# Moving VectorE's normals, low parts and the raw copies between the places of a quad of attention heads

## The chip, the cores and the metric

One Trainium2 chip; the program runs on one of its cores. The metric is the device time of one execution in microseconds, as the median over runs. Lower is better.

## What is computed

A transformer block on x of shape (8, 512, 256) in float32: layernorm, 16-head attention with l2-normalized queries and keys, an output projection, layernorm and residual; then a feed-forward block with ternary weights, layernorm and residual. Cut to what matters:

```python
q = l2norm(x @ w_q) * exp(scale);  k = l2norm(x @ w_k)      # 16 heads of 64
attn = softmax(einsum('bhid,bhjd->bhij', q, k))
out = einsum('bhij,bhjd->bhid', attn, v) @ w_out + b_out
x = x + layernorm(out)
h = silu(x1 @ w1 * s1) * (x1 @ w2 * s2)                     # x1 = layernormed x
h = gelu(h @ h1 * t1);  h = gelu(h @ h2 * t2)
x = x + layernorm(h @ w3 * s3)
```

## The kernel before

TensorE multiplies in a rounded float32 format. To keep float32 precision each operand is split in a high part (the rounded value) and a low part (what is left), and products of high with high, high with low and low with high are added up. So nearly every tile that TensorE reads has a high part, made by ScalarE or GpSimd with a copy, and a low part, made by VectorE with a subtraction.

Attention runs as a pipeline over 256 slots (two per head, `i` in the code), and a few more at its end. Eight slots, called places 0 to 7 here (`r = i % 8`), serve a quad of four heads, which is two pairs of heads: an even pair, then an odd one. There are 32 quads. Every engine has its own program: a loop over the slots, in which the order of the calls is written out by hand. Each engine works strictly in that order, and waits on semaphores.

What TensorE does in a slot: scores of slot i (L1027, L1028, into a pair of PSUM banks), values of slot i - 2 (L1044, six matmuls, reading `Ph` and `Pl`), and then, by place: in places 6, 0, 1 and 2 a projection of one tile of x to queries and keys (L986), in 3 and 4 one to values, in 0 and 5 the transposes of a pair's keys and queries ("turn", L1013), in 7 the output projection of the quad before last (`outp`, L1058). Those results go to three banks `G`, which a plan hands out in order; each user waits until the one before it on the bank is evacuated (`wait_bank`). In place 1 the projection gets the bank that held the turned keys of place 0, in place 2 that of the turned queries.

What the other engines do for it. Slot by slot ScalarE computes exp (L493) and its high part `Ph` (L498), VectorE the low part `Pl` (`p_low`, L705) of the slot before; the values matmuls one slot later want it. ScalarE squares a projected tile (L472), VectorE sums it (`head_sums`, L675), GpSimd takes the root (L362, L365, L368), VectorE scales the tile (`head_scale`, L684). Turned keys and queries are split by ScalarE (L485) and VectorE (`turn_low`, L699), then SP's queue copies them into the operand layout of the scores (`stack`, L245 and L246, 640 KB for each head of the pair; the scores wait for them, and so does the next `turn_high`).

The softmax sums go another way. ScalarE evacuates a head's values and sum (`evacuate`, L504); SP moves the sum into `Dp` (`take_sums`, L254, 2 KB); VectorE takes the reciprocal of a pair (`invert`, L713, places 7 and 3); SP stores it in HBM (`store_rec`, L259, "rows<-Rp") and reads it back spread over partitions (`spread_rec`, L266, "work<-rows"); VectorE multiplies (`normal`, L721, two instructions, a pair's result is called its normals), GpSimd copies the high part (`o_high`, L373), VectorE subtracts for the low part (`o_low`, L727), and `outp` reads both. `add_part` (L739) adds the projection to y. In place 7 VectorE does the scale of place 6's tile, then `invert`, then two `add_part`; then, in place 0, `p_low`.

ScalarE's queue also issues copies of 22 pieces of the raw feed-forward weights inside HBM (`copy_piece`, L509, 512 KB each), one at the end of place 7 of each quad up to slot 183, and 22 loads with which VectorE counts nonzero bits (`look_piece`, `count_piece`, L764), at the end of fixed slots. All SP transfers share one queue, ScalarE's another.

After the slots come the feed-forward layers (`layers`, `group`, `gate`, `halves`), for eight batches.

Of the kernel before, what the change touches and what calls it, by code (L numbers as in the profile page):

```python
# [15 lines left out]
NP = B * HP  # L16
NQ = B * 4
NU = 2 * NG
# [158 lines left out]
PIECES = 22  # L177
# [9 lines left out]

def copy_at(i):

    n, r = divmod(i - 15, 8)  # L190
    return n if r == 0 and 0 <= n < PIECES else None

# [26 lines left out]
def sync_program(q, M):  # L219
# [80 lines left out]
    for i in range(SLOTS):  # L300
        g, c, b, r, live = slot(i)
        i32_, pb = i % 32, i // 32 - 1
        if i in (5, 6):
            load_wo(i - 3)
        if i % 2 == 0 and 0 <= i // 2 - 2 < NG:
            take_sums(i // 2 - 2)
        if i % 4 == 0 and 0 <= i // 4 - 2 < NP:
            spread_rec(i // 4 - 2)
        if 0 <= pb < B - 1 and i32_ == 16:
            store_x1(pb)  # L310
        if pair_of(i) is not None:
            stack(pair_of(i), 0)
        late = 2 if i % 8 == 2 else 1
        if i >= late and i % 8 in (2, 6) and pair_of(i - late) is not None:
            stack(pair_of(i - late), 1)
        if i % 4 == 3 and 0 <= i // 4 - 1 < NP:
            store_rec(i // 4 - 1)
        if i == 3:
            load_x(1)
        if b + 2 <= B and i32_ == 31:  # L320
            load_x(b + 2)
        if 0 <= pb and i32_ == 6:
            load_xr(pb)
# [15 lines left out]
def pool_program(q, M):  # L339
# [68 lines left out]
    for i in range(SLOTS):  # L408
        g, c, b, r, live = slot(i)
        i32_, pb = i % 32, i // 32 - 1  # L410
        if b < B and i32_ == 5:
            norm_root(b + 1)
        if i % 4 == 1 and 0 <= i // 4 - 2 < NP:
            o_high(i // 4 - 2)
# [30 lines left out]
def act_program(q, M):  # L445
# [120 lines left out]
    for i in range(SLOTS):  # L566
# [20 lines left out]
        if i == NU:  # L587
            q.wait_ge("cst", 64)
            e.activation(M.pre[:, :], M.sc["s1"][:, 0:1], ACT.Silu).then_inc(S["pre"])
        if copy_at(i) is not None:  # L590
            copy_piece(copy_at(i))
        if i in LOOKS:
# [29 lines left out]
def vector_program(q, M):  # L622
# [244 lines left out]
    for i in range(NU + 1):  # L867
# [6 lines left out]
        if 0 <= i - 1 < NU:  # L874
            p_low(i - 1)
        if r == 1 and pair_of(i - 1) is not None:
            turn_low(pair_of(i - 1), 1)
            turn_low(pair_of(i - 1), 0)
        if i < 3:
            split_w(4 + i)  # L880
        if i in (5, 6, 12, 13):
            split_wo(i - 5 if i < 7 else i - 10)
        if i % 4 == 2 and 0 <= n - 3 < NP:
            o_low(n - 3)
        if i % 4 == 1 and 0 <= n - 3 < NP:
            normal(n - 3)
# [13 lines left out]
        if values_of(i) is not None:  # L900
            v_low(values_of(i))
        if r == 5 and pair_of(i) is not None:
            turn_low(pair_of(i), 1)
            turn_low(pair_of(i), 0)
        for u in tiles_of(i - 1) if i else []:
            head_scale(u)
        if r == 7 and 0 <= n - 2 < NP:
            invert(n - 2)
# [7 lines left out]
        if i == FLAG_AT + 1:  # L916
            flag()
    normal(NP - 2)
    for b in range(B):
        for n in range(3):  # L920
            for m in range(KH):
# [9 lines left out]
                elif m:  # L931
                    halves(b, n, m - 1)
                if b == 0 and n == 0 and m in (0, 1):
                    add_part(NQ - 2, m)
                if b == 0 and n == 0 and m == 2:
                    o_low(NP - 2)
# [33 lines left out]
def tensor_program(q, M):  # L970
# [171 lines left out]
    def layers(b, rounded):  # L1142

        for n in range(3):
            for m in range(KH):
                group(b, n, m, rounded)
                if b == 0 and n == 1 and m == 1:
                    outp(NQ - 1, 0)
                    outp(NQ - 1, 1)
        if b + 1 < B:  # L1150
            turn3(b + 1)
        last_tiles(b, rounded)
# [20 lines left out]
    def rest(rounded):  # L1173

        for i in range(BRANCH_AT, NU + 2):
            attention(i)
        outp(NQ - 2, 0)
        outp(NQ - 2, 1)
        for b in range(B):
            layers(b, rounded)  # L1180
# [205 lines left out]
```

## Time and profile before

| what | value |
|---|---|
| runs | 1758.13 us median of 3 (1755.85 to 1760.71) |
| the profiled execution | 1754.84 us, of which the span of its instructions is 1753.0 us |
| TensorE busy | 1701.9 us, 97% of the span |
| VectorE busy | 1179.5 us, 67% (8 tenths in most slices of the attention stage, 5 later) |
| ScalarE busy | 1009.9 us, 58% |
| GpSimd busy | 497.6 us, 28% |
| TensorE's granted clock | 0.995 of full speed |
| the chain that ended last | PE 76%, DVE 10%, DMA 6% |

PE is TensorE, DVE VectorE, ACT ScalarE, POOL GpSimd, SP the sync engine, whose instructions here only issue transfers. A row of a timeline gives the start and the length of an instruction (x2: of two together) and, in brackets, the idle time of its engine before it and what ended that. Attention takes the first 1085 us or so, the feed-forward layers the rest.

### The profile page before, as it was taken

The numbers are of one execution on the slowest core, as the hardware profiler recorded it, in microseconds if no ns is written. First come the engines' busy times: TensorE is split into PE (matmuls) and PEld (weight loads), VectorE is DVE, ScalarE is ACT, GpSimd is POOL, SyncE is SP. The second block draws the span as 40 slices with busy tenths as digits, with TensorE's granted clock in tenths as the row PEclk, the third lists the DMA queues.
The fourth block names the chain that finished last, engine by engine and source line by source line (L and its number), as shares of the span: only waits on it lengthen the run. The fifth ranks groups of instructions, "written<-read, shape, count | busy, mean of one in ns | idle before, by whom it ended". The sixth has DMA issues, their size and how long they took to land.

```text
span 1753.0 us, 24640 instructions
## 1 busy us (share of the span) xinstructions
PE 1701.9 (97%) x8578; PEld 1414.8 (81%) x8578; DVE 1179.5 (67%) x2022; ACT 1009.9 (58%) x1350; POOL 497.6 (28%) x561
## 2 busy tenths in 40 slices
PE   5999999999999999999999998999999999999998
PEld 4778888888878888888888886888888888888877
DVE  5777887887877887887887885545454545544454
ACT  4777777777777777777777775322323141323231
POOL 3533543543543543543543540000000000000000
PEclk9999999999999999999999999999999999999999
DMA  4546546546546546546546654400000000000000
GB/s 129 121 113 163 135 115 164 133 117 164 131 115 163 133 118 163 131 115 157 116 108 152 175 138 105 166 13 24 1 25 1 25 1 24 1 25 1 25 1 24
DMA packets 76780, 163.41 MB, mean 93 GB/s; under 512 B 28272, under 2 KB 28656, under 8 KB 76656
## 3 DMA queue, kind: packets, MB, share of 16 engines
q1 hardware_dynamic: 67296, 128.64, 30.9%
q10 hardware_dynamic: 8352, 29.50, 5.7%
q0 software_dynamic: 1008, 3.67, 0.5%
q8 instruction: 71, 1.16, 0.3%
q14 instruction: 53, 0.43, 0.1%
HBM read 68.97 MB, written 20.19 MB: 51 GB/s over the span
## 4 chain that ended last, share of the span: by engine, by line
PE 76%; DVE 10%; DMA 6%; issue 4%; ACT 2%; POOL 2%; SPq 1%; DVEq 0%; ACTq 0%; POOLq 0%
PE bank L1044 15%; PE pair L1121 13%; PE pair L1122 13%; PE bank L986 11%; PE pair L1027 5%; PE pair L1028 4%; PE bank L1058 4%; PE pair L1111 3%; PE pair L1112 3%; DVE Pl L705 3%; DMA rows<-Rp 3%; PE bank L1013 2%; PE bank L1138 2%; PE bank L1139 2%; DMA work<-rows 1%
## 5 line engine op out<-in xcount | busy, mean ns | idle before, releaser
L1121 PE MATMUL pair<-hh,f 128*128 128x512 f32 x1024 | 399.4, 390 | 0.7 <-DVE hl L819 0.2
L1122 PE MATMUL pair<-hl,f 128*128 128x512 f32 x1024 | 398.6, 389 | 0.0
L1044 PE MATMUL bank<-Ph,V 128*128 128x512 f32 x1024 | 366.5, 399 | 17.4 <-DVE Pl L705 12.4
L493 ACT ACTIVATE P<-pair,sh 128x1024 f32<-128x1024 f32 x256 | 286.6, 1119 | 152.3 <-PE pair L1028 136.9
L705 DVE TENSOR_TENSOR Pl<-P,Ph 128x1024 fp32r<-128x1024 f32 x256 | 313.9, 1226 | 3.1 <-ACT Ph L498 3.0
L986 PE MATMUL bank<-w,xh 128*128 128x256 f32 (+1 forms) x1024 | 289.2, 345 | 6.8 <-DVE turned L699 2.8
L543 ACT ACTIVATE hr<-pair,ct 128x512 f32<-128x512 f32 x128 | 88.3, 690 | 357.7 <-PE pair L1122 357.7
L498 ACT ACTIVATE Ph<-P 128x1024 fp32r<-128x1024 f32 x256 | 271.7, 1062 | 8.1
L1044 PEld LDWEIGHTS bank<-Ph,V 128*128 128x128 f32 x1024 | 193.4, 189 | 75.1 <-issue 23.3
L1121 PEld LDWEIGHTS pair<-hh,f 128*128 128x128 f32 x1024 | 192.2, 188 | 43.8 <-DVE hl L819 3.5
L1122 PEld LDWEIGHTS pair<-hl,f 128*128 128x128 f32 x1024 | 192.2, 188 | 39.8
L986 PEld LDWEIGHTS bank<-w,xh 128*128 128x128 f32 x1024 | 182.4, 192 | 47.2 <-issue 19.0
L1027 PE MATMUL pair<-stack 128*128 128x512 f32 x512 | 209.7, 410 | 7.4 <-issue 7.3
L365 POOL TENSOR_TENSOR rs<-ss,half 128x8 f32<-128x8 f32 x128 | 213.2, 1666 | 10.7
L815 DVE CAST hh<-hr 128x512 fp32r<-128x512 f32 x128 | 54.6, 426 | 221.4 <-ACT hr L543 216.5
L1044 PE MATMUL bank<-Pl,V 128*128 128x512 f32 x512 | 203.0, 396 | 0.0
L1028 PE MATMUL pair<-stack 128*128 128x512 f32 x512 | 202.7, 396 | 0.0
L362 POOL TENSOR_SCALAR ss<-ss 128x8 f32<-128x8 f32 x128 | 86.2, 673 | 321.5 <-DVE ss L675 319.6
L986 PE MATMUL bank<-w,xl 128*128 128x256 f32 (+1 forms) x512 | 174.4, 341 | 0.0
L819 DVE TENSOR_TENSOR hl<-hr,hh 128x512 fp32r<-128x512 f32 x192 | 132.4, 689 | 10.8 <-ACT hh L550 5.6
L684 DVE TENSOR_TENSOR qk<-bank,rs 128x512 f32<-128x512 f32 x128 | 87.5, 683 | 70.6 <-POOL rs L368 70.6
L675 DVE TENSOR_REDUCE ss<-sq 128x8 f32<-128x512 f32 x128 | 87.6, 684 | 57.5 <-ACT sq L472 55.5
(104 smaller groups left out, 2608.7 us busy)
## 6 DMA issues: line engine op xcount, KB each, us to landing
stack<-turned SPq DMA_DIRECT2D x128, 384.0 KB, 4.3
stack<-turned SPq DMA_DIRECT2D x128, 256.0 KB, 4.8
work<-rows SPq DMA_DIRECT2D x128, 128.0 KB, 2.9
raw<-in_h ACTq DMA_DIRECT2D x16, 512.0 KB, 5.0
xr<-in_h ACTq DMA_DIRECT2D x16, 512.0 KB, 3.6
f<-raw ACTq DMA_DIRECT2D x12, 512.0 KB, 5.6
f<-raw SPq DMA_DIRECT2D x10, 512.0 KB, 10.5
xt<-in_x SPq DMA_DIRECT2D x8, 512.0 KB, 4.4
```

What stands on the lines that cost most here:

```text
L365: e.tensor_tensor(rs, ss, M.half[:, :], ALU.pow).then_inc(S["rs"])
L493: e.activation(M.P[:, i % 2, :], M.SB[i % 2][:, :], ACT.Exp, bias=M.sh[:, h:h + 1]).then_inc(S["exp"])
L498: e.activation(M.Ph[:, u % 3, :], M.P[:, u % 2, :], ACT.Copy).then_inc(S["ph"])
L543: e.activation(M.hr[:, u, :], M.FB[m % 4][:, :], ACT.Gelu, scale=M.sc["t1" if n == 1 else "t2"][:, m:m + 1]).then_inc(S["ea"])
L705: e.tensor_tensor(M.Pl[:, u % 3, :], M.P[:, u % 2, :], M.Ph[:, u % 3, :].bitcast(f32), ALU.subtract).then_inc(S["pl"])
L819: e.tensor_tensor(lo, raw, hi.bitcast(f32), ALU.subtract).then_inc(S["hl"])
L986: d = e.matmul(ps, l[:, k, xs], r[:, qd, k, c0:c1], start=k == 0 and n == 0, stop=k == 1 and n == 2, skip_group_check=True)
L1027: e.matmul(ps, key, M.stack[:, k, 1, :], start=True, stop=False)
L1028: d = e.matmul(ps, key, M.stack[:, k, 2, :], start=False, stop=True)
L1044: d = e.matmul(M.OB[:, :], v, p[:, u % 3, j * 512:(j + 1) * 512], start=jt == 0 and m == 0, stop=jt == 3 and m == 2)
L1121: e.matmul(ps, w, M.hh[src][:, k, :].bitcast(to), start=k == 0, stop=False)
L1122: d = e.matmul(ps, w, M.hl[src][:, k, :].bitcast(to), start=False, stop=k == KH - 1)
```

## The change

It moves work between the places of a quad, and at the end of the attention stage; no instruction is added or taken away. `turn_low` of place 0's pair goes from VectorE's place 1 back to place 0 (except in the last quad). The even pairs' `normal` goes from place 1 to the end of place 2, their `o_low` from place 2 to place 3, GpSimd's `o_high` from place 1 to place 3. On SP the odd head's `stack` of place 6 is issued ahead of `take_sums`. The raw copies start at the end of place 0 instead of place 7, in slots 8 to 208, and skip the quads that have a `look_piece` in that slot. At the end, the normals of pair 60 move to slot 252 and those of pair 61 behind the slots, and the output projection of quad 30 goes behind the second group of the first feed-forward layer, its `add_part` and the next `o_low` one group later.

```diff
@@
-def copy_at(i):
-
-    n, r = divmod(i - 15, 8)
-    return n if r == 0 and 0 <= n < PIECES else None
+RAWS = tuple(8 * q for q in range(1, 28) if q < 8 or q % 4 != 3)
+
+
+def normal_slot(n):
+
+    return {NP - 4: NU - 4, NP - 3: NU + 1, NP - 2: NU + 1, NP - 1: NU + 5}.get(n, 4 * n + 10 - n % 2)
+
+
+def low_slot(n):
+
+    return NU - 2 if n == NP - 4 else normal_slot(n) + 1
@@ sync_program
+        if i % 8 == 6 and pair_of(i - 1) is not None:
+            stack(pair_of(i - 1), 1)
         if i % 2 == 0 and 0 <= i // 2 - 2 < NG:
             take_sums(i // 2 - 2)
@@
-        late = 2 if i % 8 == 2 else 1
-        if i >= late and i % 8 in (2, 6) and pair_of(i - late) is not None:
-            stack(pair_of(i - late), 1)
+        if i % 8 == 2 and pair_of(i - 2) is not None:
+            stack(pair_of(i - 2), 1)
@@ pool_program
-        if i % 4 == 1 and 0 <= i // 4 - 2 < NP:
+        if r in (3, 5) and 0 <= i // 4 - 2 < NP:
             o_high(i // 4 - 2)
@@ act_program
-        if copy_at(i) is not None:
-            copy_piece(copy_at(i))
+        if i in RAWS:
+            copy_piece(RAWS.index(i))
@@ vector_program
-        if r == 1 and pair_of(i - 1) is not None:
-            turn_low(pair_of(i - 1), 1)
-            turn_low(pair_of(i - 1), 0)
+        if i == NU - 7:
+            turn_low(NP - 1, 1)
+            turn_low(NP - 1, 0)
@@
-        if i % 4 == 2 and 0 <= n - 3 < NP:
+        if r == 6 and 0 <= n - 3 < NP and low_slot(n - 3) == i:
             o_low(n - 3)
-        if i % 4 == 1 and 0 <= n - 3 < NP:
+        if i == low_slot(NP - 4):
+            o_low(NP - 4)
+        if r == 5 and 0 <= n - 3 < NP and normal_slot(n - 3) == i:
             normal(n - 3)
@@
-        if r == 5 and pair_of(i) is not None:
+        if pair_of(i) is not None and i != NU - 8:
             turn_low(pair_of(i), 1)
             turn_low(pair_of(i), 0)
         for u in tiles_of(i - 1) if i else []:
             head_scale(u)
+        if r == 2 and 0 <= n - 3 < NP and normal_slot(n - 3) == i:
+            normal(n - 3)
+        if i == normal_slot(NP - 4):
+            normal(NP - 4)
+        if r == 3 and 0 <= n - 3 < NP and low_slot(n - 3) == i:
+            o_low(n - 3)
         if r == 7 and 0 <= n - 2 < NP:
             invert(n - 2)
@@
+    normal(NP - 3)
+    o_low(NP - 3)
     normal(NP - 2)
@@
-                if b == 0 and n == 0 and m in (0, 1):
-                    add_part(NQ - 2, m)
-                if b == 0 and n == 0 and m == 2:
+                if b == 0 and n == 0 and m in (1, 2):
+                    add_part(NQ - 2, m - 1)
+                if b == 0 and n == 0 and m == 3:
                     o_low(NP - 2)
@@ tensor_program
-                if b == 0 and n == 1 and m == 1:
-                    outp(NQ - 1, 0)
-                    outp(NQ - 1, 1)
+                if b == 0 and n < 2 and m == 1:
+                    outp(NQ - 2 + n, 0)
+                    outp(NQ - 2 + n, 1)
@@
-        outp(NQ - 2, 0)
-        outp(NQ - 2, 1)
```

## Rows read from the trace of the kernel before

**Rows 1.** Grouped lines of TensorE from 200 to 1050 us: busy us, mean ns | idle before.

```profile
L1044 PE MATMUL bank<-Ph,V 128*128 128x512 f32 x832 | 296.3, 397 | 8.7 <-DVE Pl L705 8.7
```

**Rows 2.** Timeline of TensorE in one quad and the next: start us, length us.

```profile
833.33 0.39 PE L1044 MATMUL bank<-Pl,V 128*128 128x512 f32 x1
833.56 0.40 PE L1044 MATMUL bank<-Ph,V 128*128 128x512 f32 x1
833.99 0.47 PE L986 MATMUL bank<-w,xh 128*128 128x512 f32 x1
...
843.85 0.40 PE L1044 MATMUL bank<-Ph,V 128*128 128x512 f32 x1
...
850.82 0.40 PE L1044 MATMUL bank<-Ph,V 128*128 128x512 f32 x1
...
858.74 0.40 PE L1027 MATMUL pair<-stack 128*128 128x512 f32 x1
...
864.28 0.39 PE L1044 MATMUL bank<-Ph,V 128*128 128x512 f32 x1
```

**Rows 3.** Timeline of VectorE in the same quad and the start of the next.

```profile
827.47 0.20 DVE L713 RECIPROCAL Rp<-Dp 128x8 f32<-128x8 f32 x1 [0.25 <-DMA Dp<-work]
...
829.91 1.22 DVE L705 TENSOR_TENSOR Pl<-P,Ph 128x1024 fp32r<-128x1024 f32 x1
...
833.16 1.28 DVE L699 TENSOR_TENSOR turned<-bank,turned 128x512 fp32r<-128x512 f32 x2
834.36 1.39 DVE L721 TENSOR_TENSOR work<-work 64x512 f32<-64x512 f32 x2
...
839.99 0.69 DVE L675 TENSOR_REDUCE ss<-sq 128x8 f32<-128x512 f32 x1 [0.69 <-ACT sq L472]
...
841.30 1.18 DVE L705 TENSOR_TENSOR Pl<-P,Ph 128x1024 fp32r<-128x1024 f32 x1
...
843.82 0.76 DVE L692 TENSOR_TENSOR V<-bank,V 128x256 fp32r<-128x256 f32 x2 [0.79 <-ACT V L479]
...
848.69 1.21 DVE L705 TENSOR_TENSOR Pl<-P,Ph 128x1024 fp32r<-128x1024 f32 x1
...
859.00 0.19 DVE L713 RECIPROCAL Rp<-Dp 128x8 f32<-128x8 f32 x1
...
860.26 1.21 DVE L705 TENSOR_TENSOR Pl<-P,Ph 128x1024 fp32r<-128x1024 f32 x1
```

**Rows 4.** Timeline of ScalarE in the same quad.

```profile
831.29 1.08 ACT L485 ACTIVATE turned<-bank 128x512 fp32r<-128x512 f32 x2
...
842.40 0.58 ACT L504 ACTIVATE work<-bank 128x512 f32<-128x512 f32 x1
```

**Rows 5.** Two transfers of the odd stack, first and last start, time to landing.

```profile
L246 SPq DMA_DIRECT2D stack<-turned x1: 609/609/609, 856.7 to 856.7; - x1
...
DMA to landing us min/median/max: 4.6/4.6/4.6
...
L246 SPq DMA_DIRECT2D stack<-turned x1: 1741/1741/1741, 660.3 to 660.3; - x1
...
DMA to landing us min/median/max: 6.3/6.3/6.3
```

**Rows 6.** Chain of waits around the quad from 662.13: start us, us, what.

```profile
657.03 5.17 DMA Dp<-work
...
662.51 4.28 DMA rows<-Rp
...
667.31 6.01 DMA work<-rows
...
676.49 0.14 issue
```

**Rows 7.** Timeline of TensorE in place 7 of a quad B.

```profile
886.88 0.47 PE L1044 MATMUL bank<-Ph,V 128*128 128x512 f32 x1 [0.36 <-DVE Pl L705]
```

**Rows 8.** Timeline of TensorE at the end of attention.

```profile
1079.37 0.47 PE L1044 MATMUL bank<-Ph,V 128*128 128x512 f32 x1 [1.61 <-DVE Pl L705]
```

## The prediction

> **What bounds the kernel now.** I read the grouped lines of TensorE first. From 200 to 1050 us it runs the attention stage almost without a hole. Its largest idle time there is 8.7 us ahead of the value matmuls (L1044), all of it put down to VectorE's low parts of P (L705) [rows 1]. So TensorE sets the time, a us counts only where TensorE waits for somebody, and the somebody is VectorE's queue, which runs in the order that the code writes.
>
> Next the timeline, for one quad of heads, the one ahead of 858.74. A matmul of 512 columns follows the one before it by .23 us (833.33 to 833.56). Then in place 1 the projection starts .43 us after the last value matmul instead of .23 [rows 2]. It needs the bank that the turned keys occupied, and their low part was computed only in this place, from 833.16 for about .68 us, so until 833.84 [rows 3]. This small wait stands in nearly every quad, and none of the big lists names it, because a matmul is shown .40 us long and so covers .17 us of any hole behind it.
>
> Last the chain of waits in a quad that went badly: rows<-Rp took 4.28 us, then work<-rows 6.01 us until 673.32; a copy of raw weights, issued at the end of place 7, ran beside the stack transfers ahead of them. The even pair's normals stood in place 1 waiting for the spread, P's low part stood behind them, and TensorE behind that, until .14 us after the low part's end at 676.49 [rows 6].
>
> **The change, part by part.** The sum is made against the profiled execution's own 1754.8 us, which is 3.3 us below the median of 1758.1. I call the quads A, B, C, D by their number modulo 4. In B the layernorm of the attention result runs (finish, out_scale, additions on GpSimd), C has two transposes of x more on TensorE, and C and D end with a count of a weight piece in place 7; D has one in place 3 too.
>
> *Turned low parts in place 0.* The two halves are evacuated by ScalarE from 831.29 for 1.08 us [rows 4], so the key part is ready near 831.9 and its low part can be done by about 832.7, a whole us before the projection wants the bank (833.79). That removes .20 us and most of the .08 us of the slower restart behind it. I take .27 x 31 quads = -8.4 us. Both ends: 0, if VectorE gets to it late, and -8.7. What hides the two operations (1.28 us): VectorE's idle time in places 0 and 1. P's low part of the quad's first slot moves 1.2 us later, to end near 834.5, and is wanted two us after that.
>
> *Raw copies out of place 7, odd stack earlier, normals later.* A copy no longer runs beside the stack transfers of place 7 and the row transfers behind them. Of the 8.7 us of idle in [rows 1] I leave 2.6 to a wait that quad B has by itself (.36 us at 886.88, in each of seven [rows 7]), 6.1 remain, and with the hidden .17 us of each and the waits of scores for their stack I estimate 9. Bounds: 4 and 11. The normals, now 3 to 4 us later in the queue, would stand even a landing like that of 673.32. The copy now starts in place 0, beside the spread of the even pair. That one lost 3 us to such a neighbour in [rows 6] and now has 5 us of room, so I cost it at nothing; without this room it would be the same 1.06 us per bad quad as now.
>
> *End.* The value matmuls at 1079.37 waited 1.61 us for a low part that stood behind the normals of pair 61 [rows 8]. These normals now stand behind the last P. With the stack of the last pair issued sooner I take -3 us, between 0 and -4. Moving the output projection of quad 30 behind two groups of the next layer changes the order of full work only: nothing.
>
> *The odd stack ahead of take_sums in place 6.* This is the part that costs. SP's queue in order of issue was: even stack (two transfers), sums (Dp), odd stack (two). Transfers of this queue land in the order of issue, however small they are: in the bad quad the Dp of 657.03, ahead of the odd stack, landed at 662.20; the second transfer of the odd stack, issued at 660.3, took 6.3 us, until 666.6; and the rows<-Rp of 662.51, 4 KB, landed at 666.79, directly behind it [rows 5, 6]. In a quad without a copy the second odd transfer was issued at 856.7 and landed after 4.6 us, at 861.3 [rows 5]. So the Dp now lands behind the odd stack, near 861.4, and 861.4 is 2.7 us into place 0 of the next quad (858.74 [rows 2]). The reciprocal (L713) of the even pair stands in VectorE's queue ahead of both add_part and of P's low part for place 1. From the reciprocal's start to the end of that low part it took 2.47 us without a count (859.00 to 861.47) and 3.66 with one (827.47 to 831.13) [rows 3]. The value matmuls of place 1 want it 5.5 us into the quad (864.28 - 858.74 [rows 2]), and start .14 us after the low part's end (the piece at 676.49 [rows 6]). So the reciprocal may start at most 2.9 us into the quad without a count and 1.7 with one. With 2.7 it is 1.0 us late behind C and D (14 quads: 14 us). Behind A and B it has .2 us left, but their turned low parts of place 5 come up to 1 us later by the next paragraph, while the quad grows by less; I take .4 x 15 = 6 us. Together +20 us. Bounds: +2, if the odd stack lands faster once issued sooner, and +26.
>
> The Trainium skill (DMA: Bandwidth & Descriptors, Queues, rings and completion order) says that each engine consumes its ring in order of issue, and that the semaphore increment lands only after every earlier write of that engine. The trace agrees with it for these transfers. The same section says that completion is "not FIFO per issuing engine", because a small transfer may use few engines; by that alone Dp might overtake, which would be rival 2 below.
>
> *Normals at the end of place 2, low part in place 3.* In place 2 VectorE now idles until the square is there (L675, 839.99, after .69 us of idle as before), and then has sums, scale, two normals (1.39, pitch 1.43), reciprocal, and the low part that place 4 wants. Before, the low part started 1.31 us after the sums and took 1.18. Now it ends at 839.99 + 1.31 + 1.43 + 1.18 = 843.91 where 843.85 - .14 = 843.71 is wanted: .20 late [rows 2, 3]. The shortened place 1 moves both sides alike. Then the low part of the normals adds .6, the idle .79 ahead of L692 is used up, and 1.24 us arrive at the low part of 848.69, which ended at 849.90 with 850.82 - .14 wanted: 1.24 - .78 - .20 = .26 more. A loses .46, D (count in place 3 instead of a statistic) about .5. In B the queue is already late (the wait of .36 at 886.88 [rows 7]), so nearly all that arrives there counts: 1.43 + .6, less the idle time that its statistics of place 2 no longer share, about 1.3. C has TensorE's transposes in place 3 and loses nothing. 7 x .46 + 7 x 1.3 + 7 x .5 = 15.8. As the .20 is the difference of two numbers near 4 I take 12, and 0 to 16 for the range.
>
> Two other engines follow the normals. GpSimd's copy of them (o_high) moves behind the root of place 2's tile and is wanted by the low part in place 3 only, 3 us later. ScalarE's evacuation in place 3 waits for the same normals. They end near 842.6 (839.99 + 1.20 for sums and scale + 1.39) instead of 835.75; the evacuation started at 842.40 and takes .58 [rows 4], so it moves by .25 us and ends at 843.2, before 843.71, when the values of place 4 want it: were the spread late, they would wait for it too. The spread waits on SP only for its own rows; the odd stack no longer stands behind the 1.4 us that SP spent on issuing Dp. All this I cost at nothing.
>
> Sum: -8.4 - 9 - 3 + 20 + 12 = +11.6 us: 1766.4 in a profiled execution, 1770 as a median.
>
> **Rivals.**
> 1. *One of the two costs does not come.* Either the reciprocal is late but the chain in places 2 to 6 holds (about 0, 1758), or that chain costs 12 and Dp little (-8, so 1750). For it: margins of .2 us. Against it: the engines' order of work is fixed.
> 2. *The other side: neither comes, the change gives what it removes.* The place is the reciprocal in place 0: if Dp lands less than 1.7 us into the quad, all 31 quads pass, and the sum is -8.4 - 9 - 3 = -20, or 1738. It needs Dp to land 1.0 us sooner than the odd stack did, which the small rows<-Rp that landed behind its neighbour speaks against [rows 5, 6].
> 3. *The copies do harm in place 0 as well:* beside the odd pair's chain they cost the .5 to 1 us in 22 quads that they cost before in place 7, and the forecast becomes 1782.
>
> **How the numbers follow.** My forecast has .45, rival 1 .25, rival 2 .2, rival 3 .1. What a measurement here can tell from no change is about .3%, 5.3 us. Slower by more: forecast and rival 3, .55. Faster by more: rival 2 and the better part of rival 1, .3. The rest, .15, is no difference. The range goes from 1740 to 1783, since cases of both signs hold much; within the forecast's own case it is 1763 to 1780.
>
> **What would show it.** In the profile after: the projection of place 1 directly behind the values (right, if the .43 is .23); idle time of L713 put down to DMA Dp<-work well over the .25 us of 827.47 in nearly every quad, and TensorE waiting for L705 in place 1 where it never did; L705 waits in place 4; no wait of L721 for work<-rows. Wrong, if Dp lands before 1.7 us into a quad, or if VectorE's idle time ahead of L675 in place 2 is gone.

## The result, and the profile after

The changed kernel takes 1802.69 us (median of 4 runs, 1801.01 to 1805.07) against 1758.25 before (4 runs): ratio 1.0254, interval 1.0235 to 1.0273, so 2.5% slower. The profiled execution took 1801.01 us, with a span of 1799.2. I had forecast 1770 and a range up to 1783: slower was right, but the loss is nearly four times what I had summed up.

The work is the same, TensorE only waits more. Of the 46.2 us by which the span grew, 14.7 stand in its busy time all the same (1701.9 before). One reason is that a matmul of 512 columns is shown .40 us long at a pitch of .23, and the first .17 us of each hole count as busy. Busy time by engine, first row of the page after:

```profile
PE 1716.6 (95%) x8578; PEld 1411.2 (78%) x8578; DVE 1178.3 (65%) x2022; ACT 1014.6 (56%) x1350; POOL 487.5 (27%) x561
```

The list of waits of TensorE over the whole span (us in total, times, longest). Before, its first rows:

```profile
PE bank L1044 <- DVE Pl L705: 12.4, 17, 1.6
...
PE bank L1044 <- ACT work L504: 4.8, 4, 2.5
...
PE bank L986 <- DVE turned L699: 2.8, 2, 2.7
```

After (lines have moved: L986, L1013, L1027 and L1044 are L1005, L1032, L1046 and L1063 now, L699, L705, L713, L721 and L739 are L708, L714, L722, L730 and L748):

```profile
PE bank L1063 <- DVE Pl L714: 16.6, 28, 1.0
PE bank L1032 <- DVE y L748: 16.3, 11, 4.1
...
PE bank L1063 <- ACT work L513: 6.2, 3, 3.6
PE bank L1005 <- DVE turned L708: 6.0, 9, 2.1
```

One waiter is new: the transposes of place 0 (L1032) wait 16.3 us for the second `add_part` (L748), whose bank they get. Before, they never waited for it. VectorE's own rows name what is behind it. The grouped lines of VectorE over the span, before and after (busy us, mean ns | idle before):

```profile
L713 DVE RECIPROCAL Rp<-Dp 128x8 f32<-128x8 f32 x64 | 12.5, 195 | 6.9 <-DMA Dp<-work 3.4 <-issue 3.2
```

```profile
L722 DVE RECIPROCAL Rp<-Dp 128x8 f32<-128x8 f32 x64 | 13.0, 202 | 99.4 <-DMA Dp<-work 88.2 <-issue 10.3
```

The reciprocal's idle time went from 6.9 to 99.4 us. How that reaches TensorE is seen in one quad, of kind C, from 915.51. VectorE:

```profile
919.85 0.20 DVE L722 RECIPROCAL Rp<-Dp 128x8 f32<-128x8 f32 x1 [3.64 <-DMA Dp<-work]
919.97 1.26 DVE L748 TENSOR_TENSOR y<-bank,bb 128x512 f32<-128x512 f32 x2
921.16 1.22 DVE L714 TENSOR_TENSOR Pl<-P,Ph 128x1024 fp32r<-128x1024 f32 x1
```

TensorE in the same quad:

```profile
915.51 0.40 PE L1046 MATMUL pair<-stack 128*128 128x512 f32 x1
...
919.02 0.39 PE L1005 MATMUL bank<-w,xh 128*128 128x512 f32 x1
920.70 1.25 PE L1032 MATMUL bank<-ident,qk 128*128 128x128 f32 x8 [1.29 <-DVE y L748]
...
923.87 0.40 PE L1063 MATMUL bank<-Ph,V 128*128 128x512 f32 x1
924.11 0.40 PE L1005 MATMUL bank<-w,xh 128*128 128x512 f32 x1
```

And SP's issues ahead of it, then the chain's rows from the last of them on:

```profile
911.24 1.36 SPq L253 DMA_DIRECT2D stack<-turned  x1
912.64 1.35 SPq L254 DMA_DIRECT2D stack<-turned  x1
914.04 1.81 SPq L262 DMA_DIRECT2D Dp<-work  x1
```

```profile
914.04 5.73 DMA Dp<-work
919.77 0.03 DVEq L35
```

Dp has 2 KB, is issued 1.5 us ahead of the quad and lands 4.3 us into it. This quad is one of the worse; over the 31 quads, Dp landed 3.0 us into the quad as a median, where it landed just at its start before. Nearly all of that difference is already in the issue. Before, Dp was issued 4.9 us ahead of the quad as a median, in the quad of 858.74 here:

```profile
853.88 1.38 SPq L254 DMA_DIRECT2D Dp<-work  x1
```

In the changed kernel it is issued 2.0 us ahead, since SP first spends 2.8 us on issuing the two transfers of the odd stack (911.24 to 914.04). From issue to landing it took 4.3 us as a median before and 4.8 now. The reciprocal starts at 919.85; the first `add_part` is done .8 us later, the transposes start at 920.70 instead of 919.25 (919.02 + .23), 1.45 us late. The last row of TensorE shows the gain as well: the projection of place 1 follows the values by .24 us, where it took .43 [rows 2].

To see where each part lands I took, for quads 1 to 30, the time from the first scores matmul of a slot to the next slot's, and added it up by place (rows of TensorE's timeline; us). The first column is the span up to slot 8; then the eight places; then places 0 and 1 of the last quad; then what is left of the span. The same table has the experiments below, each from its one profiled execution, so that a us or two of a column can be chance; verdicts rest on the medians. Two columns scatter more: the start (67.6 to 70.1), and the rest, which goes from 692.7 to 699.1 among the kernels whose end is as before. There VectorE waits for the last rows of reciprocals, and P's low part behind it: values waited 1.61 us for it before [rows 8] and 4.5 us in e11.

```
kernel                     to 8  place0    1      2      3      4      5      6      7   last 0,1  rest
before                     69.1  137.4  122.1  111.4  122.0  116.4   94.7  113.8  166.8    5.5    693.8
after                      67.6  155.9  129.5  111.4  115.2  122.4   99.4  119.7  170.8   11.5    695.8
e1_sums_first              68.1  135.7  114.2  111.3  115.2  123.1   99.4  119.6  169.5    5.5    705.1
e2_normals_back            68.3  149.9  132.5  111.4  120.8  116.4   94.7  114.0  169.9   10.6    695.8
e3_stack_first_alone       69.7  169.7  162.9  111.4  115.1  116.2   94.7  114.0  170.1   11.4    697.4
e4_turn_low_alone          68.2  137.3  114.2  111.4  126.9  116.3   94.7  113.8  168.2    5.6    692.7
e5_raws_alone              70.1  135.8  122.0  111.3  116.5  116.2   94.8  114.0  167.7    5.6    697.0
e6_end_alone               68.2  135.8  122.6  111.5  121.4  116.4   94.8  113.9  168.4    5.5    702.1
e7_late_reciprocal         68.2  137.4  115.0  111.3  119.0  125.7   99.3  119.7  173.2    5.6    703.8
e8_turn_low_and_raws       67.6  135.6  114.0  111.4  125.0  116.6   94.8  114.5  168.2    5.6    693.3
e9_sums_other_queue        67.8  136.5  115.8  111.3  115.2  121.9   99.3  119.5  170.9    5.6    705.0
e10_normals_place2_start   67.6  137.2  113.9  111.3  115.6  117.8   94.7  115.4  168.0    5.5    696.6
e11_normals_place2_end     68.2  135.8  114.2  111.4  115.2  121.9   99.4  119.8  168.7    5.5    699.1
```

After against before: places 0 and 1 +18.5 and +7.4, place 3 -6.8, places 4 to 7 +6.0, +4.7, +5.9 and +4.0, the last quad's first places +6.0, the rest +2.0, the start -1.5. That is the 46.2 us between the two spans.

### The profile page after: what moved, and what is told of

The parts are those of the page before. It is cut to its first block, busy times and chain, and to the rows that moved or that the text cites. A ratio compares the mean times of both kernels' runs of the same rounds, so it can differ in the third digit from the quotient of the medians.

```text
span 1799.2 us, 24640 instructions
## 1 busy us (share of the span) xinstructions
PE 1716.6 (95%) x8578; PEld 1411.2 (78%) x8578; DVE 1178.3 (65%) x2022; ACT 1014.6 (56%) x1350; POOL 487.5 (27%) x561
## 4 chain that ended last, share of the span: by engine, by line
PE 65%; DVE 15%; DMA 9%; issue 5%; SPq 3%; ACT 2%; POOL 1%; DVEq 0%; ACTq 0%; POOLq 0%
PE pair L1140 12%; PE pair L1141 12%; PE bank L1063 11%; PE bank L1005 9%; DMA Dp<-work 8%; DVE Pl L714 5%; PE pair L1046 3%; PE pair L1047 3%; PE pair L1130 3%; PE pair L1131 3%; DVE work L730 2%; PE bank L1032 2%; PE bank L1157 2%; PE bank L1158 2%; PE bank L1077 1%
## 5 line engine op out<-in xcount | busy, mean ns | idle before, releaser
L1063 PE MATMUL bank<-Ph,V 128*128 128x512 f32 x1024 | 371.3, 403 | 28.4 <-DVE Pl L714 16.6
L714 DVE TENSOR_TENSOR Pl<-P,Ph 128x1024 fp32r<-128x1024 f32 x256 | 315.0, 1231 | 9.0 <-ACT Ph L507 9.0
L1005 PE MATMUL bank<-w,xh 128*128 128x256 f32 (+1 forms) x1024 | 287.0, 342 | 9.6 <-DVE turned L708 6.0
L1063 PEld LDWEIGHTS bank<-Ph,V 128*128 128x128 f32 x1024 | 193.6, 189 | 105.1 <-issue 61.4
L1046 PE MATMUL pair<-stack 128*128 128x512 f32 x512 | 209.7, 409 | 8.7 <-issue 8.5
L1005 PEld LDWEIGHTS bank<-w,xh 128*128 128x128 f32 x1024 | 181.8, 191 | 41.9 <-issue 12.6
L1063 PE MATMUL bank<-Pl,V 128*128 128x512 f32 x512 | 203.1, 397 | 0.0
L1005 PE MATMUL bank<-w,xl 128*128 128x256 f32 (+1 forms) x512 | 174.1, 340 | 0.0
L371 POOL TENSOR_SCALAR ss<-ss 128x8 f32<-128x8 f32 x128 | 56.8, 444 | 423.2 <-DVE ss L684 423.2
```

Source lines behind the costliest of these rows:

```text
L714: e.tensor_tensor(M.Pl[:, u % 3, :], M.P[:, u % 2, :], M.Ph[:, u % 3, :].bitcast(f32), ALU.subtract).then_inc(S["pl"])
L1005: d = e.matmul(ps, l[:, k, xs], r[:, qd, k, c0:c1], start=k == 0 and n == 0, stop=k == 1 and n == 2, skip_group_check=True)
L1046: e.matmul(ps, key, M.stack[:, k, 1, :], start=True, stop=False)
L1063: d = e.matmul(M.OB[:, :], v, p[:, u % 3, j * 512:(j + 1) * 512], start=jt == 0 and m == 0, stop=jt == 3 and m == 2)
```

## The experiments

All ratios are against the kernel before, run on the same chip.

### e1_sums_first: the whole change, but the sums ahead of the odd stack again

```diff
@@ sync_program
-        if i % 8 == 6 and pair_of(i - 1) is not None:
-            stack(pair_of(i - 1), 1)
         if i % 2 == 0 and 0 <= i // 2 - 2 < NG:
             take_sums(i // 2 - 2)
+        if i % 8 == 6 and pair_of(i - 1) is not None:
+            stack(pair_of(i - 1), 1)
```

> The kernel after, with one line back: in place 6 SP issues the sums (Dp) ahead of the odd stack again. Theory: the Dp behind the odd stack is the largest cost; the waits of places 0 and 1 (34 us over quads 1 to 30) and the wait of the last quad's transposes (4 us) go, so about 1765 us. Rival (the normals and low parts in places 2 and 3 are the large cost, and the late reciprocal is mostly hidden): 1790 us or more.

Measured: 1764.55 us, ratio 1.0034 (1.0022 to 1.0046). Places 0 and 1 are back (135.7 and 114.2), the last quad's too, and the reciprocal hardly waits:

```profile
L722 DVE RECIPROCAL Rp<-Dp 128x8 f32<-128x8 f32 x64 | 12.8, 199 | 17.0 <-DMA Dp<-work 11.9 <-issue 4.2
```

So the order of two issues on SP costs 38 us of the 44 in this kernel. (The spans differ by 32.5 only. This execution is 4 us above its median, and the rest of its span is 9.3 us longer than the changed kernel's, for a reason that e6 shows.) Place 1 at 114.2 against 122.1 before is the gain of the turned low parts, no longer covered up. What stays of the loss stands in places 4 to 7 and in the rest, which grew by 11.3.

### e2_normals_back: the whole change, but the even pairs' normals and low parts in places 1 and 2

```diff
@@ normal_slot
-    return {NP - 4: NU - 4, NP - 3: NU + 1, NP - 2: NU + 1, NP - 1: NU + 5}.get(n, 4 * n + 10 - n % 2)
+    return {NP - 4: NU - 4, NP - 3: NU + 1, NP - 2: NU + 1, NP - 1: NU + 5}.get(n, 4 * n + 9)
@@ vector_program
-        if r == 6 and 0 <= n - 3 < NP and low_slot(n - 3) == i:
+        if r in (2, 6) and 0 <= n - 3 < NP and low_slot(n - 3) == i:
             o_low(n - 3)
...
-        if r == 5 and 0 <= n - 3 < NP and normal_slot(n - 3) == i:
+        if r in (1, 5) and 0 <= n - 3 < NP and normal_slot(n - 3) == i:
             normal(n - 3)
...
-        if r == 2 and 0 <= n - 3 < NP and normal_slot(n - 3) == i:
-            normal(n - 3)
...
-        if r == 3 and 0 <= n - 3 < NP and low_slot(n - 3) == i:
-            o_low(n - 3)
```

`o_high` goes back with them; the end of attention stays as changed.

> The kernel after, with the even pairs' normals back in place 1, their low parts in place 2 and GpSimd's high part in place 1 (the last quads as in the kernel after). Theory: the 20 us of waits in places 4 to 7 go, but the spread of the reciprocals now lands 8 to 12 us into the quad, while the normals are wanted at 7.5 us, so place 3 waits again in the quads with a copy, up to 2.3 us in each of 22: 1785 to 1830 us. Rival (the two moves are independent, and the late reciprocal costs only its own wait): 1783 us.

Measured: 1785.6 us, ratio 1.0152 (1.0125 to 1.0179), 17 us below the changed kernel. Places 4, 5 and 6 go back to 116.4, 94.7 and 114.0, so what they lost is the normals' doing. Place 0 is 6.0 below the changed kernel. Place 3 rises by 5.6 and place 1 by 3.0; the normals wait for their rows again, 14.9 us in total against 2.8 in the changed kernel, behind a spread that starts from a late reciprocal. By the total time independence and a weak tie between the two costs can't be told apart.

### e3_stack_first_alone: before, with only the odd stack ahead of the sums in place 6

```diff
@@ sync_program
+        if i % 8 == 6 and pair_of(i - 1) is not None:
+            stack(pair_of(i - 1), 1)
         if i % 2 == 0 and 0 <= i // 2 - 2 < NG:
             take_sums(i // 2 - 2)
@@
-        late = 2 if i % 8 == 2 else 1
-        if i >= late and i % 8 in (2, 6) and pair_of(i - late) is not None:
-            stack(pair_of(i - late), 1)
+        if i % 8 == 2 and pair_of(i - 2) is not None:
+            stack(pair_of(i - 2), 1)
```

> The kernel before, with only the odd stack of place 6 issued ahead of the sums. Theory: the reciprocal waits for its Dp until 2 to 3 us into each quad, places 0 and 1 pay about 34 us, and the normals in place 1 wait for a late spread on top: 1790 to 1815 us. Rival (the order on SP does not matter by itself, as the transfers are all short): below 1765 us.

Measured: 1832.35 us, ratio 1.0413 (1.0386 to 1.044), more than any theory gave, and 30 us above the whole change. The waits of TensorE:

```profile
PE bank L987 <- DVE turned L700: 29.6, 31, 3.3
PE bank L1014 <- DVE y L740: 28.0, 27, 4.4
PE bank L1045 <- DVE Pl L706: 20.7, 26, 3.8
```

All three readers behind the reciprocal now hold TensorE up, place 1 most of all (162.9 against 122.1), where the normals and the turned low parts stand. In the whole change the normals stand a place later, so the late spread behind the late reciprocal has time to land. The copies are another part: here they still start at the end of place 7, beside the odd stack, and in quads 1 to 23 Dp took 6.0 us on average and landed 3.9 us into the quad, against 4.8 and 2.9 in the changed kernel, and place 0 is .67 us longer than there; in quads 24 to 30, behind e3's last copy, the two kernels are within .25 us in all three. So the single parts don't add up. By the ratios e3 +73, e4 -6, e5 -9, e6 +4 and the normals +12 (e11 against e8) make +74 us, the change +45.

### e4_turn_low_alone: before, with the turned low parts in place 0

```diff
@@ vector_program
-        if r == 1 and pair_of(i - 1) is not None:
-            turn_low(pair_of(i - 1), 1)
-            turn_low(pair_of(i - 1), 0)
+        if i == NU - 7:
+            turn_low(NP - 1, 1)
+            turn_low(NP - 1, 0)
@@
-        if r == 5 and pair_of(i) is not None:
+        if pair_of(i) is not None and i != NU - 8:
```

> The kernel before, with only the turned low parts of place 0 moved back into place 0 (the last pair's excepted). Theory: the projection of place 1 starts .27 us earlier in 31 quads: 1750 us. Rival (VectorE gets to them late or delays P's low part, so nothing is won): 1758 us.

Measured: 1753.64 us, ratio .9965 (.9951 to .9979): 4.7 us by the medians and 6.2 by the ratio, where the theory wanted 8. Place 1 gave 7.9 us, .26 for each quad, as summed up; but place 3 took 4.9 back. My reading is that with place 1 shorter, the spread (which has its own pace) comes later against the slots, and so do the normals in place 1 and what stands behind them; e10 and e11, where the normals stand later, bring place 3 down to 115 us. In this kernel itself it isn't shown: the normals' wait for their rows is 7.6 us in total, against 9.4 before.

### e5_raws_alone: before, with only the raw copies moved to place 0

```diff
-    n, r = divmod(i - 15, 8)
-    return n if r == 0 and 0 <= n < PIECES else None
+RAWS = tuple(8 * q for q in range(1, 28) if q < 8 or q % 4 != 3)
@@ act_program
-        if copy_at(i) is not None:
-            copy_piece(copy_at(i))
+        if i in RAWS:
+            copy_piece(RAWS.index(i))
```

> The kernel before, with only the raw copies moved from the end of place 7 to place 0. Theory: the reciprocals' rows no longer stand beside a copy, but their spread does; 4 to 6 us of waits in places 3 and 0 go: 1752 to 1754 us. Rival (one collision is exchanged for another): 1758 us.

Measured: 1752.87 us, ratio .9951 (.9934 to .9967). Place 3 gave 5.5 us of it. The span of the profiled execution is only 1.9 us below before: the kernel before has a median of 1761.41 us beside e5's runs, but its profiled execution took 1754.84. So the copies do no harm in place 0, and rival 3 of the prediction falls.

### e6_end_alone: before, with only the end of attention as changed

```diff
 def normal_slot(n):
+    return {NP - 4: NU - 4, NP - 3: NU + 1, NP - 2: NU + 1, NP - 1: NU + 5}.get(n, 4 * n + 9)
@@ vector_program
+        if i == normal_slot(NP - 4):
+            normal(NP - 4)
@@
+    normal(NP - 3)
+    o_low(NP - 3)
     normal(NP - 2)
```

The moves of the last low parts, of `o_high` and of quad 30's output projection are in it too, as in the diff of the change.

> The kernel before, with only the changes at the end: normals of pair 60 in slot 252, those of pair 61 behind the slots, the output projection of quad 30 behind the second group of the first layer. Theory: the evacuation of slot 251 waits for the normals of pair 60, which now stand behind P's low part of slot 251, and the values of slot 252 wait for the evacuation: 5 to 10 us slower at the end, 1763 to 1768 us. Rival (as the prediction had it, the end gains): 1755 us.

Measured: 1762.72 us, ratio 1.0024 (1.0012 to 1.0037): a small loss where I had -3 us. The wait of the values for the evacuation:

```profile
PE bank L1058 <- ACT work L512: 12.0, 4, 6.7
```

against 4.8 in four before. In the changed kernel the place is this, the timeline of all engines at the end of attention:

```profile
1108.71 0.20 DVE L722 RECIPROCAL Rp<-Dp 128x8 f32<-128x8 f32 x1 [3.62 <-DMA Dp<-work]
...
1111.09 1.40 DVE L730 TENSOR_TENSOR work<-work 64x512 f32<-64x512 f32 x2
...
1112.58 0.60 ACT L513 ACTIVATE work<-bank 128x512 f32<-128x512 f32 x1 [3.31 <-DVE work L730]
...
1113.33 0.77 PE L1063 MATMUL bank<-Ph,V 128*128 128x512 f32 x1 [3.62 <-ACT work L513]
```

ScalarE's evacuation of the values of slot 251 overwrites a buffer that the normals of pair 60 read (`evacuate` waits for their count). Those normals were moved to slot 252, behind P's low part, and the values of slot 252 want the evacuated bank. Moving the normals at the end took the 1.61 us of [rows 8] away, and put 3.62 us in slot 252.

The expectation named this chain, but not what sets its length. Before, pair 60's normals stood in slot 249, ahead of pair 61's reciprocal; now they stand behind it and behind P's low parts. The reciprocal's 3.62 us of idle time come out again as TensorE's 3.62. In e6 it is the same with more:

```profile
1069.67 0.20 DVE L721 RECIPROCAL Rp<-Dp 128x8 f32<-128x8 f32 x1 [6.88 <-DMA Dp<-work]
```

This Dp took 7.6 us to land in e6 and 8.7 in e1, against 3.9 before and 4.2 in the changed kernel; why it differs so much stays open. It is one reason why the rest grew by 8.3 us in e6 and 11.3 in e1 and by 2.0 only in the changed kernel. The other is that the last quad is held up there for 6.0 us already, in which a wait of 2.5 us in slot 250 is gone.

### e7_late_reciprocal: the whole change, with the reciprocal behind P's low part of place 0

```diff
@@ vector_program
         if 0 <= i - 1 < NU:
             p_low(i - 1)
+        if r == 0 and 0 <= n - 3 < NP:
+            invert(n - 3)
@@
-        if r == 7 and 0 <= n - 2 < NP:
-            invert(n - 2)
```

> The kernel after, with the even pair's reciprocal moved behind P's low part of the next place 0 in VectorE's queue; SP still issues the odd stack ahead of the sums. Theory: the late Dp costs only by what stands behind the reciprocal (both add_part, whose banks the next transposes want, and the low part for place 1). With these ahead of it the waits of places 0 and 1 go although Dp lands as late as before: 1765 to 1772 us. Rival (Dp's lateness costs through the spread and the normals behind it, or the SP queue itself is late): above 1790 us.

Measured: 1778.22 us, ratio 1.0104 (1.0082 to 1.0125). Dp is as late as in the changed kernel (2.9 us into the quad as a median, 3.0 there), but places 0 and 1 are within 2 us of e1, so nothing but the place of the reciprocal in VectorE's queue made them wait. It is above the theory's 1765 to 1772: places 3, 4 and 7 are 3.8, 2.6 and 3.7 us longer than in e1. I put that down to the spread, which still starts late; it was not tried by itself.

### e8_turn_low_and_raws: before, with e4 and e5 together

```diff
@@ act_program
-        if copy_at(i) is not None:
-            copy_piece(copy_at(i))
+        if i in RAWS:
+            copy_piece(RAWS.index(i))
@@ vector_program
-        if r == 1 and pair_of(i - 1) is not None:
+        if i == NU - 7:
             turn_low(NP - 1, 1)
             turn_low(NP - 1, 0)
@@
-        if r == 5 and pair_of(i) is not None:
+        if pair_of(i) is not None and i != NU - 8:
```

> The kernel before, with turned low parts in place 0 and the raw copies in place 0, and nothing else. Theory: the place 1 gain (8 us) and the removal of the collisions in place 7 add up, as the normals in place 1 wait for the spread only sometimes: 1742 to 1748 us. Rival (the copy now collides with the spread in place 0, and the normals in place 1 stand waiting for it; only the late normals would make room): 1755 us or more.

Measured: 1747.95 us, ratio .9933 (.9917 to .995). By the ratios the gains of 6.2 and 8.6 us make 11.8 together, so they nearly add up. By place they don't: place 3 is at 125.0, against 116.5 with the copies alone, which takes back all that place 1 gave, and what is left between e8 and e5 stands in the start and the rest of the span (2.5 and 3.7 us). Both columns scatter by as much. The normals' wait for their rows has grown to 19.1 us in total, from 9.4. So with the normals in place 1, place 3 is what the shorter place 1 runs into.

### e9_sums_other_queue: the whole change, the even pair's second Dp issued by GpSimd

```diff
@@ sync_program
-        if i % 2 == 0 and 0 <= i // 2 - 2 < NG:
+        if i % 2 == 0 and (i % 8 != 6 or i >= NU - 2) and 0 <= i // 2 - 2 < NG:
             take_sums(i // 2 - 2)
@@ pool_program
+        if i % 8 == 6 and i < NU - 2 and 0 <= i // 2 - 2 < NG:
+            take_sums(i // 2 - 2)
```

GpSimd's program gets the same `take_sums`, and VectorE's `invert` waits for its semaphore (not shown).

> The kernel after, with the even pair's second Dp of place 6 issued from GpSimd's queue instead of SP's (the last quad's excepted). Theory: what makes it late is that it stands behind 640 KB of the same queue; on another queue it lands before the odd stack and the reciprocal waits under .5 us: 1765 to 1775 us. Rival (all 16 engines are full of the odd stack, so another queue's small transfer is as late): 1795 us or more.

Measured: 1771.5 us, ratio 1.0068 (1.0046 to 1.009); 31 us of the 44 are gone. VectorE's row:

```profile
L737 DVE RECIPROCAL Rp<-Dp 128x8 f32<-128x8 f32 x64 | 12.7, 199 | 18.1 <-DMA Dp<-work 17.1
```

So a Dp in time is enough. But the run doesn't say what had made it late, since not only the queue has changed. GpSimd needn't wait for SP's four stack issues: it issued Dp 7.4 us ahead of the quad as a median, and in 24 of the 31 quads ahead of both transfers of the odd stack. It then landed before the quad began. In a quad B, for one, ahead of all four, it took 1.7 us to land:

```profile
886.35 0.64 POOL L419 DMA_DIRECT2D Dp<-work  x1
```

In the other seven, all behind an A, GpSimd is late with its own work, and Dp is issued after the first transfer of the odd stack. SP's issues, then GpSimd's:

```profile
854.44 1.36 SPq L253 DMA_DIRECT2D stack<-turned  x1
855.84 1.39 SPq L254 DMA_DIRECT2D stack<-turned  x1
```

```profile
855.79 0.64 POOL L419 DMA_DIRECT2D Dp<-work  x1
...
DMA to landing us min/median/max: 4.9/4.9/4.9
```

There Dp took 4.9 to 6.2 us, as long as in SP's own queue (4.8 as a median), and landed 2.0 us into the quad (3.3 in one), .8 us or more ahead of the stack's last transfer. So the expectation's rival, that another queue's small transfer is as late beside the stack, is nearly right where it could be seen. In the other quads the gain comes with an issue ahead of the odd stack, as in e1, and says nothing of the queue.

### e10_normals_place2_start: e8, with the even pairs' normals at the start of place 2

```diff
@@ vector_program
-        if i % 4 == 2 and 0 <= n - 3 < NP:
+        if r == 6 and 0 <= n - 3 < NP:
             o_low(n - 3)
-        if i % 4 == 1 and 0 <= n - 3 < NP:
+        if r in (2, 5) and 0 <= n - 3 < NP:
             normal(n - 3)
@@
         for u in tiles_of(i - 1) if i else []:
             head_scale(u)
+        if r == 2 and 0 <= n - 3 < NP:
+            o_low(n - 3)
@@ pool_program
-        if i % 4 == 1 and 0 <= i // 4 - 2 < NP:
+        if r in (2, 5) and 0 <= i // 4 - 2 < NP:
             o_high(i // 4 - 2)
```

> The kernel before, with turned low parts and raw copies in place 0, and the even pairs' normals in place 2 directly behind P's low part, ahead of the sums, into VectorE's wait for the square; their low part behind the scale of the same place. Theory: the spread gets 4 us more room, so the 8 us of waits in place 3 go, and the low part for place 4 starts under .2 us later than before and is in time: 1738 to 1743 us. Rival (any move of the normals into place 2 makes the queue late for place 4): 1748 us or more.

Measured: 1744.04 us, ratio .9898 (.9877 to .9918), the fastest kernel here, 1% below before, and a us above the theory's range. The normals stand right behind P's low part of their slot and ahead of the sums, where VectorE idled for the square before (.69 us at 839.99 [rows 3]). Place 3 is 115.6; places 4 and 6 lose 1.4 and 1.6 us only.

### e11_normals_place2_end: e8, with the normals where the change puts them

```diff
@@ pool_program, against e8
-        if i % 4 == 1 and 0 <= i // 4 - 2 < NP:
+        if r in (3, 5) and 0 <= i // 4 - 2 < NP:
             o_high(i // 4 - 2)
@@ vector_program
-        if i % 4 == 2 and 0 <= n - 3 < NP:
+        if r == 6 and 0 <= n - 3 < NP:
             o_low(n - 3)
-        if i % 4 == 1 and 0 <= n - 3 < NP:
+        if r == 5 and 0 <= n - 3 < NP:
             normal(n - 3)
@@
         for u in tiles_of(i - 1) if i else []:
             head_scale(u)
+        if r == 2 and 0 <= n - 3 < NP:
+            normal(n - 3)
+        if r == 3 and 0 <= n - 3 < NP:
+            o_low(n - 3)
```

> The same, with the normals at the end of place 2 and their low part in place 3, as in the kernel after (SP's order and the end of the stage as before). Theory: the waits of places 4 to 7 cost 20 us, the room for the spread gives back 8: 1758 to 1762 us. Rival (the place within place 2 does not matter): the same time as with the normals at its start.

Measured: 1760.81 us, ratio .9999 (.9986 to 1.0012). Against e10, places 4 to 6 are 4.1, 4.7 and 4.4 us longer and place 3 is the same (115.2). The medians are 17 us apart: 14 of them are in places 4 to 7, and the rest in the start and the end, which scatter. Three things differ between the two kernels: the normals stand ahead of the sums or behind the scale, their low part in place 2 or 3, and GpSimd's copy of them likewise. Which of these counts for how much was not tried.

## Why the prediction was right about the sign and wrong about the size

**Turned low parts in place 0: right.** Predicted -8.4 us, place 1 gave 7.9 in e4 and in e1 (122.1 to 114.2). That place 3 takes back 4.9 of it in e4, and all of it in e8, was not in the sum; in the changed kernel, with the even pairs' normals out of place 1, place 3 takes nothing back.

**Collisions: right in kind, a little high.** Predicted -9, place 3 gave 6.8, of which the copies alone give 5.5 (e5). The waits of the normals for their rows (L721, now L730) fell from 9.4 to 2.8 us in total.

**The odd stack ahead of the sums: mechanism right, the term mis-sized. This is the step that failed.** I took +20 us, with 26 as the upper bound; it costs 20.2 in place 0 and 15.3 in place 1 of quads 1 to 30 and 6.0 in the last quad (after against e1), 41.5 in all, and 38 in the medians. By kinds, behind C and D I had 14 us and it was 13.4; behind A and B I had 6 and it was 22.1; and the last quad's 6.0 I hadn't counted. Three things in my working:

1. The landing. I took 2.7 us into the quad from one transfer for all. Dp did land behind the odd stack in every quad, and 2.7 was near the median of 3.0, but the reciprocal's start in the changed kernel was 3.0 to 4.2 us into the quad behind A, 2.2 to 4.3 behind B, 2.3 to 3.6 behind C and 1.8 to 3.9 behind D, and behind quad 0 and quads 28 to 30 Dp landed 5.2 to 6.2 us into the next. Against my own limits (2.9 without a count, 1.7 with one) these starts give .8 to 1.0 us a quad for every kind.
2. A and B counted as nearly safe, at .4 us. Read as places 0 and 1 of the next quad against e1, the delay cost 1.73 us behind A (1.12 and .60), 1.04 behind B, .98 behind C (.14 and .84) and .94 behind D (.27 and .67). The kinds with a count were at the 1.0 that I had; the others cost 4.3 and 2.6 times my .4.
3. The readers. I priced one of the instructions behind the reciprocal, the low part that the values of place 1 want. The transposes of place 0 want the bank of `add_part` before that. In the quad at 915.51 both give the same limit: the transposes are wanted at 919.25 and start .85 us after the reciprocal, which leaves it 2.9 us. In B the two limits add up, since the two statistics (1.1 us) stand ahead of the turned low parts there and the projection of place 1 waits for those as well, as here in TensorE's timeline of a quad B:

```profile
888.55 0.47 PE L1005 MATMUL bank<-w,xh 128*128 128x512 f32 x1 [0.50 <-DVE turned L708]
```

The last quad, which I had not counted, is short in places 0 and 1 (5.5 us together) and took the full delay, 6.0.

The Trainium skill (DMA: Bandwidth & Descriptors, Queues, rings and completion order) says that a DMA engine takes turns between the queues that have work for it, packet by packet, and serves each ring in order of issue. The trace agrees with the second: in all 31 quads Dp landed behind the last transfer of the stack that it was issued behind, by .15 to 1.4 us. The first is not shown apart by any run, since GpSimd's Dp was mostly issued ahead of the stack (e9). "Not FIFO per issuing engine" didn't show for these transfers, so rival 2 fell: the earliest Dp landed 1.7 us into its quad.

**Normals in place 2, low parts in place 3: the working was better than my discount.** I worked out 15.8 and took 12. The lengths of places 4 to 7, after against before, grew by 20.6, of which 18.1 are in e11, without a late Dp. By kind, after less before in places 4 to 7: A .58 (I had .46), B 1.39 (1.3), D .70 (.5), C .05 (0). The .20 us of place 4 is there, as the difference of two numbers near 4:

```profile
592.29 1.39 DVE L730 TENSOR_TENSOR work<-work 64x512 f32<-64x512 f32 x2
593.72 0.20 DVE L722 RECIPROCAL Rp<-Dp 128x8 f32<-128x8 f32 x1
593.84 1.17 DVE L714 TENSOR_TENSOR Pl<-P,Ph 128x1024 fp32r<-128x1024 f32 x1
```

```profile
594.02 0.39 PE L1046 MATMUL pair<-stack 128*128 128x512 f32 x1
...
595.11 0.47 PE L1063 MATMUL bank<-Ph,V 128*128 128x512 f32 x1
```

VectorE's low part ends at 595.01, the values start at 595.11, 1.09 us after the scores, where four matmuls of .23 take .93. The list of waits shows no row for most of these: a hole of .16 us hides behind the .40 us for which a matmul is shown.

**End: wrong in sign.** Predicted -3, e6 shows +4.3 (ratio 1.0024). I had looked at what stood behind the moved normals, and neither at who waits for them to be done nor at the reciprocal that they now stand behind.

**Rivals.** None of the three came. Rival 1 needed one of the two costs to stay away, and both came; the copies of rival 3 gave a gain in place 0 (e5).

**What stays open.** Why the landings scatter by a us from quad to quad (behind A, four starts at 3.0 to 3.1 and two at 4.2, for one) was not settled. Part of it is regular: behind quads 0, 5, 10 and so on up to 30 Dp landed 1.0 to 1.4 us behind the stack's last transfer, behind all others .1 to .5. Nor was it settled whether the late issue or the 640 KB ahead in the queue holds Dp back: e1 and e3 change both at once, e9 does so in most quads, and e7 neither. e4's loss in place 3 was read from the place sums and not tried by itself.

## What to carry to other kernels

Where transfers share a queue, a small one that somebody waits for goes ahead of the large ones; count the time of the large ones' issues as well as their landing. Another queue helped here because another engine could issue it sooner. Before moving it, list everything that stands behind its reader in that engine's order, not only the next thing wanted. Take the landing from many quads and not from one, since the margin was as large as its scatter. When an instruction moves later, ask also who waits for it to be finished: a buffer's next writer can hold up more than the instruction itself did. And an instruction belongs ahead of an engine's idle time, not behind it: e10, with the normals and their low part put there, is 17 us faster than e11.

## What the runs showed of the hardware

SP issues one transfer after the other, and each issue holds it: 1.36 and 1.35 us for the two of the odd stack at 911.24 and 912.64, and 1.81 us for the 2 KB behind them. Those 2 KB took 5.73 us to land behind the stack. From GpSimd's queue 2 KB took 1.7 us when issued ahead of the stack (886.35 in e9), and 4.9 us when issued behind three of its four transfers (855.79).

After TensorE's idle time at the end of attention its granted clock was half of full speed for a while, which makes the 3.62 us cost more than they say. Windows of the changed kernel (busy us and count of PE, PEld, DVE, ACT, POOL, then PE's granted clock, DMA share, GB/s):

```profile
1107.00:1109.50 2.50, 2.37 (x11) 1.48 (x9) 0.79 (x2) 2.18 (x2) 0.00 (x0) 1.00 0.98 243
1109.50:1113.00 3.50, 0.21 (x1) 0.00 (x0) 2.96 (x4) 0.42 (x1) 0.45 (x1) 0.99 0.87 200
1113.00:1116.40 3.40, 3.08 (x7) 2.48 (x8) 1.10 (x1) 2.24 (x3) 0.17 (x1) 0.50 0.61 170
1116.40:1120.00 3.60, 3.21 (x14) 2.25 (x12) 0.58 (x2) 2.66 (x4) 0.00 (x0) 1.00 0.18 65
```

TensorE ran at full clock up to 1109.5, was idle but for .21 us until 1113.0, then ran at .50 (1.2 of 2.4 GHz) until about 1116.4: 7 matmul rows in 3.4 us, 14 in the 3.6 us behind.
